# Issuing the K/V stage's scratch stores from GpSimd instead of SyncE, in a cross-attention and dequantised feed-forward kernel

## What is computed

```python
def attention(query, ctx):                      # 32 query heads, 8 key/value heads, width 128
    q = rope(query @ wq); k = rope(ctx @ wk); v = ctx @ wv
    p = softmax(q @ k.T / sqrt(128) + mask)     # every 4 query heads share one key/value head
    return (p @ v) @ wo

def ffn(x):
    w = lut4[row, code]                         # 4-bit codes from bit planes, (1024, 1024)
    return x @ w.T + bias

x = x + attention(layernorm(x), ctx)            # x, ctx: (8, 256, 1024) float32
x = x + ffn(layernorm(x))
```

## Time and profile before

| | us |
|---|---|
| median of 3 runs | 2518.31 (2516.89 to 2518.34) |
| the profiled execution's own time | 2517.62 |
| its span in the trace | 2515.8 |

### The profile page before, as it was taken

How to read it: one execution, slowest core, us unless ns; L and a number is a source line. 1 busy time by engine, 2 the same in 40 slices (tenths; PEclk the granted TensorE clock), 3 DMA queues, 4 the chain that set the end, 5 groups by cost and what they waited for, 6 DMA issues and landing times.

```text
span 2515.8 us, 35971 instructions
## 1 busy us (share of the span) xinstructions
PE 2468.2 (98%) x13056; PEld 2108.4 (84%) x13056; DVE 1497.0 (60%) x3569; ACT 1139.5 (45%) x2485; POOL 451.6 (18%) x678
## 2 busy tenths in 40 slices
PE   8999998999999999999999999999999999999999
PEld 7888897888888888888888888888888888887887
DVE  7768776456565555656565555555555555555454
ACT  5555443454545454545454444444444444443110
POOL 1000000222222222222222222222222222221211
PEclk9999999999999999999999999999999999999999
DMA  7556556322222322222236422122221221223211
GB/s 241 182 173 193 163 182 224 128 76 84 67 76 74 93 67 77 73 82 71 73 114 194 170 59 72 51 67 63 72 65 54 72 59 59 60 67 133 106 72 51
DMA packets 243727, 255.37 MB, mean 102 GB/s; under 512 B 15584, under 2 KB 187872, under 8 KB 243552
## 3 DMA queue, kind: packets, MB, share of 16 engines
q1 hardware_dynamic: 243552, 253.08, 31.6%
HBM read 181.73 MB, written 71.30 MB: 101 GB/s over the span
## 4 chain that ended last, share of the span: by engine, by line
PE 87%; DVE 4%; DMA 3%; ACT 2%; issue 1%; SPq 1%; POOL 0%; ACTq 0%; DVEq 0%; POOLq 0%
PE bank L707 27%; PE bank L774 27%; PE bank L724 7%; PE bank L808 7%; PE bank L757 7%; PE bank L745 4%; PE bank L675 3%; PE bank L656 3%; DMA w_scratch<-small_split 1%; DVE residual L1330 1%; DMA x_scratch<-raw 1%; PE bank L625 1%; DVE residual L1315 1%; DMA ln_row<-in_L_xattn_wo 0%; DVE small_split L1284 0%
## 5 line engine op out<-in xcount | busy, mean ns | idle before, releaser
L774 PE MATMUL bank<-weights_split,small_split 128*128 128x512 f32 x3072 | 769.6, 399 | 2.4 <-DVE small_split L1516 2.4
L707 PE MATMUL bank<-acts_split,weights_split 128*128 128x512 f32 (+1 forms) x3264 | 750.6, 380 | 3.4 <-DMA acts_split<-x_scratch 3.4
L707 PEld LDWEIGHTS bank<-acts_split,weights_split 128*128 128x128 f32 x3264 | 574.9, 190 | 103.4 <-DMA acts_split<-x_scratch 3.8
L774 PEld LDWEIGHTS bank<-weights_split,small_split 128*128 128x128 f32 x3072 | 557.9, 188 | 113.7 <-DVE small_split L1516 3.5
L1623 POOL TENSOR_SCALAR probs<-probs,row_numbers 128x256 f32<-128x256 f32 x512 | 238.7, 479 | 1404.1 <-DVE row_numbers L1506 1404.1
L1066 ACT ACTIVATE probs<-probs,row_numbers 128x256 f32<-128x256 f32 x512 | 256.4, 502 | 475.7 <-DVE row_numbers L1501 475.2
L1495 DVE CUSTOM_DVE_ANT_0 probs<-bank,mask_tile 128x256 f32<-128x256 f32 x512 | 196.9, 422 | 210.3 <-PE bank L724 208.6
L1616 POOL TENSOR_TENSOR rope_x<-rope_x,sin_t 128x512 f32<-128x512 f32 (+1 forms) x136 | 167.7, 1233 | 458.9 <-ACT rope_x L1037 458.2
L724 PEld LDWEIGHTS bank<-small_split 128*128 128x128 f32 x1536 | 219.0, 191 | 27.0 <-issue 5.8
L724 PE MATMUL bank<-small_split 128*128 128x256 f32 x1536 | 225.5, 283 | 6.6 <-issue 4.7
L1462 DVE SCALAR_TENSOR_TENSOR rope_a<-bank,cos_t 128x512 f32<-128x512 f32 (+1 forms) x136 | 89.8, 660 | 216.8 <-ACT rope_x L1037 216.8
(11 more groups left out here) (107 smaller groups left out, 2386.6 us busy)
## 6 DMA issues: line engine op xcount, KB each, us to landing
raw<-in_L_xattn_wq SPq DMA_DIRECT2D x61, 512.0 KB, 4.7
raw<-in_L_xattn_wo SPq DMA_DIRECT2D x61, 512.0 KB, 3.5
k_scratch<-small_split SPq DMA_DIRECT2D x64, 256.0 KB, 2.2
v_scratch<-small_split SPq DMA_DIRECT2D x32, 512.0 KB, 2.9
x_scratch<-raw SPq DMA_DIRECT2D x64, 256.0 KB, 2.8
acts_split<-x_scratch SPq DMA_DIRECT2D x32, 512.0 KB, 7.0
small_split<-k_scratch SPq DMA_DIRECT2D x64, 256.0 KB, 2.6
mask_tile<-in_mask_BxSxS_ff SPq DMA_DIRECT2D x64, 256.0 KB, 3.4
```

The source lines that it names most:

```text
L707: last = pe.matmul(query_bank(j)[:, 0:wide], wq_s[:, h, c, a, :], xT[:, c, m, b * S:b * S + wide], start=c == 0 and i == 0, stop=c == C - ...
L774: last = pe.matmul(out_ps[part][:, :], o_s[:, a, u % 2 * S + t * P:u % 2 * S + (t + 1) * P], wo_s[:, h, m, n * BANK:(n + 1) * BANK], start ...
```

## The change

The stores of the K/V stage are taken out of SyncE's program and written into GpSimd's, in the same order among themselves and with the same waits: 64 key stores, 32 value stores, 16 weight stores and 36 row stores (18 half rows). GpSimd issues them through its own DMA queue. The loads stay with SyncE in their old order and no longer stand behind the stores' waits. In batch 0 GpSimd's multiplications by sines are interleaved with the key stores; the last tile's D0 and D1 are stored by GpSimd between the sines of the first two query heads and the first `normalize`. Row stores of the attention stage stay with SyncE and get a semaphore of their own (`late_x_stored`), since a semaphore now counts one queue. The extra 16 that three semaphores started with is dropped, and waits for zero stores with it.

```diff
@@ SyncE, batch
                 for g in range(HKV):
-                    sp.wait_ge(rope_lo, 2 + b * HKV + g + 1)
-                    sp.dma_start(k_scr[g, b], k_stage[:, g % 2].bitcast(F32)
-                                 .rearrange("p l n -> p (l n)")).then_inc(k_stored[g % 2], 16)
                     if first and A_SLOTS + 2 + g < A_PIECES:
                         load_split(A_SLOTS + 2 + g)
...
-                    if g == 0 and b - 1 in V_ROW:
-                        store_row(V_ROW[b - 1], 1)
-                    if not first and g == 1:
-                        store_weights(b - 1, D0)
-                    if not first and g == 3:
-                        store_weights(b - 1, D1)
...
-                    store_row(K_ROW[b], 0)
-                store_values(V0, 0, 0)
...
-                store_values(V2, 0, 1)
...
-                store_values(V3, 1, 1)
-                if last:
-                    sp.wait_ge(w4_ready, NB)
-                    store_weights(b, D0, True)
-                    store_weights(b, D1, True)
-                else:
+                if not last:
                     sp.wait_ge(dq_step, b * DQ_STEPS + LEAF7)
                     sp.dma_start(lut_t, lut_v[b + 1]).then_inc(lut_in, 16)
@@ ScalarE, row halves
-                act.wait_ge(x_stored, 2 * 16 * (2 * e + j))
+                if e < A_ROWS or e == A_ROWS and j == 0:
+                    wait_stored(x_stored, 2 * (2 * e + j))
+                else:
+                    wait_stored(late_x_stored, 2 * (2 * (e - A_ROWS) + j))
@@ GpSimd
-            for g in range(HKV):
-                pool.wait_ge(rope_in, 2 + g + 1)
-                pool.tensor_tensor(ropes[g % 2][0], ropes[g % 2][0], sin_t[:, :], ALU.mult).then_inc(rope_sind, 1)
+            def store_row(e, j):
+
+                pool.wait_ge(x_lo, 2 * e + j + 1)
+                dst = x_scr[e // HT, e // REP % 2, 4 * j:4 * j + 4].rearrange("c p l (t n) -> t l p c n", n=P)
+                for l in range(2):
+                    done = pool.dma_start(dst[e % REP, l], raw_t[:, l * BANK:(l + 1) * BANK]
+                                        .rearrange("p (c n) -> p c n", n=P))
+                    done.then_inc(x_stored, 16)
...
+            def store_weights(tile, i, last=False):
+                pool.wait_ge(stage_lo, STAGED // 2 + staged_count(tile, i))
+                stage, stored = staging(i, last)
+                dst = w_scr.rearrange("p j k (t n) -> t j p k n", n=P)
+                pool.dma_start(dst[tile, i - D0], stage.bitcast(F32).rearrange("p (k n) -> p k n", n=P)
+                             ).then_inc(stored, 16)
+
+            def batch(b, first=False, last=False):
+
+                for g in range(HKV):
+                    if first:
+                        pool.wait_ge(rope_in, 2 + g + 1)
+                        pool.tensor_tensor(ropes[g % 2][0], ropes[g % 2][0], sin_t[:, :],
+                                           ALU.mult).then_inc(rope_sind, 1)
+                    pool.wait_ge(rope_lo, 2 + b * HKV + g + 1)
+                    pool.dma_start(k_scr[g, b], k_stage[:, g % 2].bitcast(F32)
+                                   .rearrange("p l n -> p (l n)")).then_inc(k_stored[g % 2], 16)
+                    if g == 0 and b - 1 in V_ROW:
+                        store_row(V_ROW[b - 1], 1)
+                    if not first and g == 1:
+                        store_weights(b - 1, D0)
+                    if not first and g == 3:
+                        store_weights(b - 1, D1)
+                if b in K_ROW:
+                    store_row(K_ROW[b], 0)
+                store_values(b, V0, 0, 0)
+                if b in K_ROW:
+                    store_row(K_ROW[b], 1)
+                store_values(b, V1, 1, 0)
+                store_values(b, V2, 0, 1)
+                if b in V_ROW:
+                    store_row(V_ROW[b], 0)
+                store_values(b, V3, 1, 1)
...
             query_sin(0)
             query_sin(1)
+            store_weights(NB - 1, D0, True)
+            store_weights(NB - 1, D1, True)
             for u in range(NU):
                 normalize(u)
```

More of the change, by code:

```diff
@@ L245, in build_xattn_ffn @@
         v_stored = sem("v_stored")
-        x_stored, res_stored, out_stored = sem("x_stored"), sem("res_stored"), sem("out_stored")
+        x_stored, late_x_stored = sem("x_stored"), sem("late_x_stored")
+        res_stored, out_stored = sem("res_stored"), sem("out_stored")
         ident_step, ident_ok = sem("ident_step"), sem("ident_ok")
@@ L354, in load_row @@
                 sp.dma_start(ln_row[:, :], x_tiles[e]).then_inc(row_in, 16)
[L356 to L363, removed]
             def load_turned(hf, j, c):
@@ L431, in batch @@
             def batch(b, first=False, last=False):
[L433 to L444, removed]
                 if not first:
@@ L845, in context_high, with wait_stored @@
                                ACT.Copy).then_inc(ctx_hi, 1)
+            def wait_stored(stored, count):
+                if count:
+                    act.wait_ge(stored, 16 * count)
             def row_mean(e):
@@ L931, in weights_high @@
                     act.wait_ge(w4_tr, tile * 2 + i - D0 + 1)
-                    act.wait_ge(v_stored, 16 * (tile * len(V_TURNS) + V_TURNS[i] + 1))
+                    wait_stored(v_stored, tile * len(V_TURNS) + V_TURNS[i])
                     act.activation(staging(i)[0][:, 0:BANK], w4_ps[i - D0][:, :], ACT.Copy).then_inc(stage_hi, 1)
@@ L1073, in turned_high @@
                 if u == 0:
[L1074 to L1075 removed]
+                    wait_stored(k_stored[0], NB * K_SLOT0 + 1)
+                    wait_stored(v_stored, NB * len(V_TURNS) - 1)
                 act.wait_ge(pT_tr, 2 + u + 1)
@@ L1118, in _ @@
                     act.wait_ge(w_lo, A_PIECES + PIECE_AT[max(at for at in PIECE if at <= u)] + 1)
-                    act.wait_ge(x_stored, 4 * 16 * ROW_AT[u + 1])
+                    if ROW_AT[u + 1] == A_ROWS:
+                        wait_stored(x_stored, 4 * A_ROWS)
+                    else:
+                        wait_stored(late_x_stored, 4 * (ROW_AT[u + 1] - A_ROWS))
                     row_square(ROW_AT[u + 1], [raw_t[:, n * BANK:(n + 1) * BANK] for n in range(2)])
@@ L1597, in _ @@
         def _(pool):
-            for s in range(2):
-                pool.sem_inc(k_stored[s], 16)
-            pool.sem_inc(v_stored, 16)
             pool.memset(ident[:, :], 0.0).then_inc(ident_step, 1)
@@ new lines, in store_values @@
+            def store_values(b, i, t, n):
+                pool.wait_ge(stage_lo, STAGED // 2 + staged_count(b, i))
+                stage, stored = staging(i)
+                pool.dma_start(v_scr[b, t, :, :, n * BANK:(n + 1) * BANK].rearrange("l p n -> p l n"),
+                               stage.bitcast(F32).rearrange("p (l n) -> p l n", l=2)).then_inc(stored, 16)
+            def store_weights(tile, i, last=False):
[4 more added lines that the diff above has]
+                             ).then_inc(stored, 16)
@@ L1612, in query_sin @@
+            batch(0, first=True)
+            for b in range(1, NB - 1):
+                batch(b)
+            batch(NB - 1, last=True)
             def query_sin(j):
```

37 lines of the change are left out of this document (17 added, 20 removed).

## The result

| | us |
|---|---|
| changed kernel, median of 4 runs | 2544.36 (2543.7 to 2545.87) |
| kernel before, median of 4 runs beside it | 2518.28 |
| ratio | 1.0108, 95% interval 1.0096 to 1.012 |
| profiled execution of the changed kernel, its span | 2544.83, 2542.9 |

The changed kernel is 26 us slower; the prediction was 33 slower (2551 us), in a range of 2511 to 2605. The direction and the size are near, but the sum behind them is not: an issue on GpSimd costs a fraction of what it was given, and most of the loss comes from something that the prediction had set aside.

What follows compares the result with a forecast made beforehand. The prediction saw TensorE bound by store-landing latency, with no slack behind D0. Its terms, 17 + 3 + 2 + 2 + 6 + 3 = +33 us on 2517.6, gave 2551 us; range for 8 times in 10: 2511 to 2605.

Steps and rivals of the forecast that it cites:

- The price of an issue: GpSimd's time to issue a store: 0.43 us + 2.9 ns a run, 0.8 us for a key, 3.4 for D0.
- Rival A: Dear end: GpSimd issues cost 5.9 ns a run and bound batches 1 to 3; +86, 2604 us; chance 0.22.
- The flat price: Every GpSimd store issue costs the same whatever its runs; at 0.8 us, -4, 2513 us; chance 0.13.
- What SyncE no longer does ... gives nothing more: Loads: dropping SyncE's waits in front of them gains nothing; the passage's are held by DMA engines and TensorE's last read.
- At 0.4 more they still do: Key stores: must land within about 3.6 us, take 2.2; at 0.4 us more they still land in time.
- D0, +17: Weight store D0, batches 1 to 7: lands 2.4 us later, with no slack before TensorE; 7 x 2.4 = +17 us.
- Batch 0, +2: Batch 0: key 0's store lands sooner in its own queue, -3.3 us; later sine products cost 6.6, partly hidden; together +2.
- The rows, +2: Row half 0's stores, batches 1 to 3: 5.6 us to landing against 5.55 now; +2 us for the three.
- The clock, +6: TensorE's clock: seven waits growing to about 3 us, half of some 1.6 us lost behind each; +6 us.
- Queueing, +3: GpSimd, batches 2 to 4: the V row's second half issues just ahead of D0; +1 us each, +3.
- the passage, +3: Passage to attention: last tile's D0 and D1 take 6.8 us to issue, delaying `normalize` by 2.6 us, say +3.
- Rival C: GpSimd's descriptor writing holds up VectorE, each batch 7 us longer on top; 33 + 49, 2600 us; chance 0.09.

Runs made afterwards that it cites:

- e1: Changed kernel, with SyncE holding the loads at the start of batches 1 to 7 until the previous batch's V3 store has landed: 2529.31 us, ratio 1.0042.
- e2: Kernel before, all DMAs on SyncE, with the next batch's loads issued just ahead of V3's store: 2533.21 us, ratio 1.0058.
- e4: Changed kernel, with GpSimd storing D0 before key 1 and not behind it: 2525.78 us, ratio 1.0027.
- e5: Kernel before, all DMAs on SyncE, with D0 stored before key 1 and not behind it: 2512.14 us, ratio 0.998.
- e3: Changed kernel, with GpSimd making the next sine product ahead of each key store in batch 0: 2542.22 us, ratio 1.0092.
- e7: Kernel before, with D0 stored before key 1 and batch 0's key 0 store ahead of the loads of weight pieces 8 and 9: 2512.42 us, ratio 0.998.
- e6: Changed kernel with loads held for V3's store, D0 before key 1, and sines ahead of batch 0's key stores: 2517.11 us, ratio 0.9995.

## Why the prediction was near, and where its steps failed

**The price of an issue.** Failed. It was put at 0.43 us + 2.9 ns a run, from the nearest row of GpSimd's work, and is 0.51 us + 0.4 ns. The cheap end held. The Trainium skill ("DMA: Bandwidth & Descriptors", section on the anatomy of a DMA on the gpsimd path) says that many descriptors can be emitted before their incremental cost shows up; the trace agrees, with 0.90 us for 1024 runs. Rival A is out with it. An instruction that computes on columns was the wrong neighbour for one that writes out a transfer.

**The flat price did not give its time either.** The prediction's own formula, 14p - 15.5, gives -4 us at p = 0.8, 2513 us. Measured are 2544. Between them stand 31 us that the formula lacked.

**"What SyncE no longer does ... gives nothing more."** This is the step that failed and carries the most. It asked only whether earlier loads gain anything and not what they delay. SyncE's wait for V3's low part, which the change removes, was also what kept 1 MB of loads behind a 512 KB store that the next batch's first key waits for. Shown by e1 and e2, 15 us, of which 11 to 13 in batches 2 to 6. The Trainium skill ("DMA: Bandwidth & Descriptors", section on issuing engines not being separate DMA queues) says that DMAs of all engines run on the same sixteen DMA engines and interleave. The trace agrees: key 0's store, alone in its own queue, still took 7.4 us to land in batch 0 (issued at 18.67, ScalarE released at 26.07), and 7.5 in SyncE's queue behind the loads (18.89 and 26.36).

**"At 0.4 more they still do."** Failed too. The prediction let key stores land later for nothing. They land 0.5 us later in the median, and ScalarE's wait for them rises from 7.5 to 17.6 us, in nine waits. How much of the time that is, no run separates.

**D0, +17.** Its landing was to move by 2.4 us in each of seven batches. Its time from issue to landing did not move at all; the issue moved, by about 0.7 us in batch 5: GpSimd starts it later and key 1's issue ahead of it is longer. "No slack between the landing of D0 and TensorE" was right and is why any delay ahead of it, V3's above all, comes out in full: e4 gets 18.6 us by moving this one store. Right mechanism, wrong source of the delay.

**Batch 0, +2.** It came out at +1.3 by the stretches, against a batch that had a lower clock before, and at about +3 against the same batch in e5; neither half is what was written. The -3.3 for a queue of its own did not come: ScalarE still waits 2.06 us for key 0's store and TensorE 2.16 us, and key waits follow later. The sines' 6.6 us came in full (VectorE's waits from 2.8 to 10.0) and cost 2 at most, by e3.

**The rows, +2.** ScalarE waits 19.2 us in place of 19.9, TensorE 6.4 in place of 6.7: about nothing, near the forecast.

**The clock, +6.** Right in kind and a little low. In six of seven batches behind the first the granted clock is 0.97 against one before, and in batch 5 the level of 1.2 GHz costs 1.5 us behind one wait. TensorE's busy time for the same work is up by 8.6 us in all.

**Queueing, +3, and the passage, +3.** Neither was seen. GpSimd waited for the low part ahead of each of its 64 key and 32 value stores, so it was never behind. In the passage it issues D0 and D1 in 1.82 us instead of 6.8 and then waits another 2.17 us for its first `normalize`; the passage is 0.8 us shorter. (Two slips in the working change nothing: batch 1 has six row stores and not eight, and two keys in 6.03 us are 3.0 us each.)

**Rival C.** VectorE's busy time is unchanged. There is a collision, the other way round and small: an issue of GpSimd's that falls beside VectorE's L1293 takes longer. In batch 5 the issue at 296.62 takes 0.88 us instead of 0.56 and ends 0.11 us after VectorE's 0.81 us do. All 15 key stores that took 0.88 or 0.89 us start 0.03 to 0.05 us behind an L1293. The Trainium skill ("SBUF — State Buffer", section on two separate sides) describes such a case: while VectorE runs an instruction in a two-port mode, GpSimd cannot write a DMA's descriptors. The trace agrees in the form and has 0.3 us for the size; whether L1293 runs in such a mode no row says. Over 64 key stores it is the mean of 0.64 us against the median of 0.56, 5 us of issues. What of it reaches the time is not shown.

So 2551 against 2544 is in part luck: some 12 us of a price that does not exist (17, less about 7 x 0.7 by which the issue does come later) stood in for 15 us of an order that was not looked at.

## What to carry to other kernels

In this kernel the order of one queue was also a priority. Whoever moves stores to another queue has to ask of each load that stood behind a store's wait: when will it start now, and whose landing does it share the DMA engines with. And of the transfers ready at one moment, put first the one that somebody waits for: two such swaps on one queue (D0 ahead of key 1, the row store ahead of the next row's load) gave 10 us where a second queue lost 26, and an edit that only shifts the burst of loads by one store (e7) gives nothing.

## What the runs showed that was not expected

GpSimd issues 1024 runs in 0.90 us and 128 in 0.56. From the end of V3's low part to the issue of its store it needs 0.30 us in batch 5 (284.99 to 285.29); SyncE, before, needed 0.02 (267.09 to 267.11). The wait of 2.15 us in batch 5 was followed by matmuls at the lower clock level, 7.50 us for 48; the same 48 behind waits of 0.3 us and of 0.79 us take 6.0. But behind a wait of 2.16 us in batch 0 the granted clock stayed at 1.00 and they took 6.32, so the length of one wait does not settle it. Open stays how the last 5 us between e6 and e5 divide, and what the early row load and the longer waits for key stores cost.
